# Cross attention: three of four maximum products ahead of the scores, the fourth row strip's scores first, softmax sums copied out of PSUM and divided a step later

## The chip, the cores and the metric

The kernel runs on one core of a Trainium2 chip. The metric is the device time of one execution in microseconds (us), lower is better. Five engines work side by side: TensorE (PE in the profile; its weight loads are PEld), VectorE (DVE), ScalarE (ACT), GpSimd (POOL) and SyncE (SP, which only starts transfers here). They meet through semaphores. TensorE writes to PSUM alone, which has eight banks of 128 partitions x 512 fp32 numbers.

## The reference

The program is a small network on a latent array `x` of 32 batches x 64 rows x 256 channels: cross attention to a context, self attention, a mixture of experts, cross attention again, a Mamba block in two directions and a second feed-forward block. The change touches only the cross attention, which runs twice (as `x0` and `x1`). Cut to what matters, with 16 heads of width 16 and 1601 context rows of 128 channels:

```python
q = (layernorm(x) @ Wq + bq)          # 64 queries in each of 32 batches
k = ctx @ Wk + bk                     # 1601 keys
v = ctx @ Wv + bv
scores = einsum('bhqd,bhkd->bhqk', qh, kh) / sqrt(16)
attn = softmax(scores, axis=-1)
out = einsum('bhqk,bhkd->bhqd', attn, vh)
x = x + concat(out) @ Wo + bo
```

## The kernel before, in words

The 1601 keys of a batch are 13 tiles of 128 (the last has 65), taken two at a time: a batch `u` is seven steps `g` = 0 to 6, and step `s` = 7u + g. Steps 0 to 5 hold two key tiles, step 6 one of 65 keys. A layer has 224 steps.

The softmax is written with keys on the partitions. Its shift, a maximum over keys for each head and query, is therefore made one batch ahead from products with queries on the partitions. Operations are named by a letter:

- **M** (`largest`, L476): the product of rounded queries with 512 rounded keys of the next batch, one for each of four row strips `j` of the array (partitions 32j to 32j+31). VectorE takes its maximum (`keep_max`, L692).
- **K** (`project_keys`, L463) and **V** (`project_values`, L494): projections of keys (for the next step's M) and of values (two steps ahead). ScalarE copies them out (L604, L612). GpSimd rounds the copied keys (`round_keys`, L654) before an M may use them, and splits the context (`split_context`, L367 and L369).
- **scores** (L544): 16 fp32 products, four for each strip, into four PSUM banks `score_ps`, one bank to a strip; then one product a strip that adds the shift (L550). ScalarE takes the exponential in two halves, strips 0 and 1, then 2 and 3 (L630), with the K copy between the halves and the V copy after them. `score_ps` is not doubled: scores wait for both exponentials of the step before.
- **P** (`weigh`, L526): probabilities times values; VectorE adds the result up (`gather`, L722 and L725).
- **S** (`spread_sums`, L502) at step 1: the softmax sums of the batch before, spread over partitions; VectorE divides by them (`divide`, L707 and L709).
- **T** (`turn_maxes`, L484) at step 6: the shift. **W** (`project_out`, L509), every second batch: the output projection; VectorE adds it to `x` (L714).

All but the scores share four PSUM banks, `misc_ps`, in rotation: an operation takes the bank of the fourth operation before it in the list `ORDER`, and `open_bank` waits until that one has been read, by ScalarE for K and V and by VectorE for the rest. Each engine takes its instructions in written order. The fixed order of TensorE in a full step is: scores, M0, M1, K, V, M2, M3, P.

```python
def bank(op):
    return misc_ps[:, AT[op] % NMB, :]
if AT[op] >= NMB:
    read_out(pe, ORDER[AT[op] - NMB])
```

Of the kernel before, what the change touches and what calls it, by code (L numbers as in the profile page):

```python
# [261 lines left out]
def cross_attention(nc, tag, x_sb, ident, x_sel, pair_mask, ctxT, wq, wk, wv, wo, bq, bv, bo):  # L262
# [15 lines left out]
    def cols(i):  # L278
        return slice(i * P, i * P + keys(i))
# [13 lines left out]
    def step_ops(s):  # L293

        u, g = divmod(s, NG)
        early = QUADS if g == NG - 1 else QUADS // 2
        maxima = [("M", u + 1, g, j) for j in range(QUADS)] if u + 1 < B else []
        ops = maxima[:early]
        if key_share(u, g)[0] < B:
            ops.append(("K",) + key_share(u, g))  # L300
        if s + 2 < STEPS:
            ops.append(("V", s + 2))
        ops += maxima[early:]
        if g == NG - 1 and u + 1 < B:
            ops.append(("T", u + 1))
        if s > 0:
            ops.append(("P", s - 1))
        if g == 1 and u > 0:
            ops.append(("S", u - 1))
        if g == 2 and u % 2 == 0 and u > 0:  # L310
            ops.append(("W", u // 2 - 1))
        return ops
# [10 lines left out]
    with ExitStack() as ctx:  # L323
# [75 lines left out]
        u_sb = sb(f"{tag}_u", [P, 2, GROUPS, LQ])  # L399
        oT = sb(f"{tag}_oT", [P, GROUPS, 2, LQ])  # L400
        recip = sb(f"{tag}_recip", [P, GROUPS * LQ])
        bias = sb(f"{tag}_bias", [P, D])
# [12 lines left out]
        score_ready = [sem(f"{tag}_score_ready{ph}") for ph in range(2)]  # L415
        exp_done = sem(f"{tag}_exp_done")
        o_done = sem(f"{tag}_o_done")
        bias_done = sem(f"{tag}_bias_done")
# [23 lines left out]
        def _(pe):  # L442
# [89 lines left out]
            def scores(s):  # L532
# [6 lines left out]
                if s > 0:  # L539
                    pe.wait_ge(exp_done, 2 * s)  # L540
                for n, (h, c) in enumerate(parts):
                    for j in range(QUADS):
                        rows = slice(j * 32, (j + 1) * 32)
                        nc.tensor.matmul(score_ps[0:kn, j, n * P:(n + 1) * P], kT[rows, u % 2, c, cols(mine[h])],  # L544
                                         qz[rows, u % 2, c, :, :].rearrange("p s q -> p (s q)"),
                                         start=n == 0, stop=False, skip_group_check=True)
                if g == 0:
                    read_out(pe, ("T", u))
                for j in range(QUADS):
                    nc.tensor.matmul(  # L550
                        score_ps[0:kn, j, 0:len(mine) * 2 * P], ones[j * 32:j * 32 + 1, 0:kn],
                        shift[j * 32:j * 32 + 1, u % 2, :].rearrange("p (a n) -> p a n", a=1).broadcast_to([1, len(mine), 2 * P]),
                        start=False, stop=True, skip_group_check=True).then_inc(score_ready[j // 2], 1)

            pe.wait_ge(w_in, 16 * NW)
# [14 lines left out]
            for s in range(STEPS):  # L570
                u, g = divmod(s, NG)
                early = QUADS if g == NG - 1 else QUADS // 2
                scores(s)
                if u + 1 < B:
                    for j in range(early):
                        largest(("M", u + 1, g, j))
                if key_share(u, g)[0] < B:
                    project_keys(("K",) + key_share(u, g))
                if s + 2 < STEPS:
                    project_values(("V", s + 2))  # L580
                if u + 1 < B:
                    for j in range(early, QUADS):
                        largest(("M", u + 1, g, j))
                if g == NG - 1 and u + 1 < B:
# [3 lines left out]
                if g == 1 and u > 0:  # L588
                    spread_sums(("S", u - 1))
                if g == 2 and u % 2 == 0 and u > 0:  # L590
                    project_out(("W", u // 2 - 1))
# [93 lines left out]
        def _(dve):  # L685
# [10 lines left out]
            def keep_shift(op):  # L696
# [5 lines left out]
                nc.vector.tensor_copy(shift[:, b % 2, :], bank(op)[:, 0:2 * P]).then_inc(dve_free, 1)  # L702

            def divide(op):
                b = op[1]
                made(dve, op)
                nc.vector.reciprocal(recip[:, :], bank(op)[:, 0:GROUPS * LQ]).then_inc(dve_free, 1)  # L707
                read_out(dve, op)
                nc.vector.tensor_tensor(oT[:, :, b % 2, :], u_sb[:, b % 2, :, :],  # L709
                                        recip[:, :].rearrange("p (r q) -> p r q", q=LQ), ALU.mult).then_inc(o_done, 1)  # L710
# [31 lines left out]
            for s in range(STEPS):  # L742
                u, g = divmod(s, NG)
                if u + 1 < B:
                    for j in range(QUADS):
                        keep_max(("M", u + 1, g, j))
                if g == NG - 1 and u + 1 < B:
                    keep_shift(("T", u + 1))
                if s > 0:
                    gather(("P", s - 1))  # L750
                if g == 1 and u > 0:
                    divide(("S", u - 1))
                if g == 2 and u % 2 == 0 and u > 0:
                    add_out(("W", u // 2 - 1))
            gather(("P", STEPS - 1))
            divide(("S", B - 1))
            add_out(("W", B // 2 - 1))

# [1403 lines left out]
```

## Time and profile before

| | |
|---|---|
| median of 3 runs | 4311.27 us (4309.27 to 4313.52) |
| the profiled execution | 4310.48 us, of it the span 4308.7 us |
| PE busy | 3776.3 us, 88% of the span |
| DVE busy | 2804.7 us, 65% |
| ACT busy | 1979.2 us, 46% |
| POOL busy | 1519.9 us, 35% |
| steps of the first cross attention | 85 to 1143 us of the span |
| steps of the second | 1978 to 3036 us |

An engine's share of busy time is an average over stages that differ. A busy TensorE is not one at its peak, since the records of its products overlap. What matters in a step is which engine's work ends last before the next step can begin.

### The profile page before, as it was taken

What the parts mean: (1) busy time and instruction counts of PE and PEld (TensorE: products, weight loads), DVE (VectorE), ACT (ScalarE), POOL (GpSimd) and SP (SyncE); (2) the same over time, 40 slices, a digit from 0 to 9 for tenths busy, and PEclk for the clock granted to TensorE, in tenths of its full rate; (3) what the DMA queues carried; (4) which work ended last, traced back from release to release, by engine and by line L of the source; (5) the groups of instructions that cost most, each with busy time, mean ns of one, the idle gap of its engine ahead of it and who ended that gap; (6) DMA issues with size and microseconds to landing.
All of it is one profiled execution on the core that took longest, in us unless ns stands there. A gap on an engine that the chain in (4) does not pass through costs nothing. (4 is left out here: it accounts for less than half of the span.)

```text
span 4308.7 us, 129527 instructions
## 1 busy us (share of the span) xinstructions
PE 3776.3 (88%) x54334; PEld 2632.0 (61%) x54335; DVE 2804.7 (65%) x4729; ACT 1979.2 (46%) x2986; POOL 1519.9 (35%) x1445
## 2 busy tenths in 40 slices
PE   6999999999798299948999999999877878878788
PEld 4777777777688166626777777777423333323357
DVE  5666666666466212235666666666779999999964
ACT  2555555555422122214555565555444444444432
POOL 3333323333100200043333333332047777888710
PEclk8999999999899599968999999999979999999989
DMA  1001000000000600120100010000012222222200
GB/s 63 26 26 34 26 26 26 27 33 18 10 0 2 252 28 30 32 71 25 33 26 26 26 32 28 26 26 11 25 49 69 71 72 72 79 76 70 70 33 20
DMA packets 79937, 182.53 MB, mean 42 GB/s; under 512 B 10755, under 2 KB 31267, under 8 KB 79043
## 3 DMA queue, kind: packets, MB, share of 16 engines
q1 hardware_dynamic: 76354, 166.58, 12.3%
q8 instruction: 413, 6.77, 0.6%
q0 software_dynamic: 3072, 8.39, 0.6%
q14 instruction: 98, 0.80, 0.1%
HBM read 157.37 MB, written 17.56 MB: 41 GB/s over the span
## 5 line engine op out<-in xcount | busy, mean ns | idle before, releaser
L692 DVE TENSOR_REDUCE x_maxes<-x_misc_ps 128x1 f32<-128x512 f32 (+1 forms) x1792 | 1044.7, 628 | 569.1 <-PE x_misc_ps L476 568.8
L630 ACT ACTIVATE x_probs<-x_score_ps 128x1024 f32<-128x1024 f32 (+1 forms) x896 | 859.8, 961 | 795.6 <-PE x_score_ps L550 789.2
L654 POOL CAST x_kT_hi<-x_kT 128x512 fp32r<-128x512 f32 (+1 forms) x448 | 257.9, 576 | 1454.3 <-PE x_misc_ps L494 971.1
L1679 PE MATMUL b_acc_ps<-b_read,ident 128*128 128x512 f32 x1024 | 566.1, 683 | 187.3 <-POOL b_read L1765 153.8
L1757 POOL TENSOR_TENSOR b_drive<-b_b_all,b_dtx 128x1024 f32<-128x1024 f32 x256 | 602.5, 2354 | 331.2 <-DVE b_dtx L1837 280.7
L1799 DVE TENSOR_TENSOR_SCAN b_state<-b_decay_ps,b_drive 128x512 f32<-128x512 f32 x512 | 606.7, 1205 | 12.5 <-POOL b_drive L1757 12.5
L1747 ACT ACTIVATE b_decay_ps<-b_dt,b_a_neg 128x504 f32<-128x504 f32 x512 | 350.0, 685 | 461.9 <-DVE b_state L1799 461.9
L1679 PEld LDWEIGHTS b_acc_ps<-b_read,ident 128*128 128x128 f32 x1024 | 193.9, 211 | 505.9 <-POOL b_read L1765 257.2
L544 PE MATMUL x_score_ps<-x_qz,x_kT 32*128 32x128 f32 x13312 | 494.1, 283 | 5.9 <-ACT x_probs L630 5.9
L526 PE MATMUL x_misc_ps<-x_probs,x_v 128*32 128x64 f32 x26624 | 464.8, 221 | 0.5 <-issue 0.5
L526 PEld LDWEIGHTS x_misc_ps<-x_probs,x_v 128*32 128x32 f32 x26624 | 392.6, 110 | 103.8 <-issue 87.6
L544 PEld LDWEIGHTS x_score_ps<-x_qz,x_kT 32*128 32x128 f32 x13312 | 405.5, 182 | 70.6 <-issue 31.2
L476 PE MATMUL x_misc_ps<-x_kT_hi,x_qz_hi 32*128 32x512 f32 (+1 forms) x2048 | 425.9, 400 | 5.1 <-POOL x_kT_hi L654 4.1
L604 ACT ACTIVATE x_kT<-x_misc_ps 128x512 f32<-128x512 f32 (+1 forms) x448 | 247.9, 553 | 158.6 <-PE x_misc_ps L463 155.1
L612 ACT ACTIVATE x_v<-x_misc_ps 128x512 f32<-128x512 f32 (+1 forms) x448 | 255.6, 570 | 12.5 <-PE x_misc_ps L494 12.5
L476 PEld LDWEIGHTS x_misc_ps<-x_kT_hi,x_qz_hi 32*128 32x128 f32 x2048 | 208.1, 186 | 84.3 <-DVE x_maxes L692 21.5
L463 PE MATMUL x_misc_ps<-x_raw_hi,x_wk_hi 128*128 128x512 f32 (+1 forms) x512 | 229.5, 448 | 34.0 <-POOL x_raw_lo L369 15.4
L1809 DVE TENSOR_TENSOR b_read<-b_c_ps,b_state 128x512 f32<-128x512 f32 x384 | 253.7, 661 | 0.0
L494 PE MATMUL x_misc_ps<-x_wv_hi,x_raw_hi 128*128 128x256 f32 (+1 forms) x832 | 241.1, 290 | 0.3
L369 POOL TENSOR_TENSOR x_raw_lo<-x_raw,x_raw_hi 128x512 fp32r<-128x512 f32 (+1 forms) x192 | 235.1, 1225 | 15.5
L494 PE MATMUL x_misc_ps<-x_wv_hi,x_raw_lo 128*128 128x256 f32 (+1 forms) x832 | 233.8, 281 | 0.0
L494 PE MATMUL x_misc_ps<-x_wv_lo,x_raw_hi 128*128 128x256 f32 (+1 forms) x832 | 233.5, 281 | 0.0
(281 smaller groups left out, 5593.3 us busy)
## 6 DMA issues: line engine op xcount, KB each, us to landing
x_raw<-in_ctxT SPq DMA_DIRECT2D x64, 800.5 KB, 4.4
b_b_all<-b_bc_rows SPq DMA_DIRECT2D x128, 256.0 KB, 3.5
b_c_all<-b_bc_rows SPq DMA_DIRECT2D x128, 256.0 KB, 3.1
m_w<-in_m_w SPq DMA_DIRECT2D x16, 704.0 KB, 19.2
m_w<-in_m_w SPq DMA_DIRECT2D x8, 768.0 KB, 19.8
m_slot_rows<-m_zero SPq DMA_DIRECT2D x1, 4992.0 KB, 17.4
m_block_rows<-m_slot_rows SPq DMA_DIRECT2D x39, 128.0 KB, 2.0
m_slot_out<-m_out SPq DMA_DIRECT2D x39, 128.0 KB, 1.7
```

What stands on the lines that cost most here:

```text
L476: ins = nc.tensor.matmul(dst[:, m * kn:(m + 1) * kn], qz_hi[rows, b % 2, c, :, :].rearrange("p s q -> p (s q)"), kT_hi[rows, (b * NG + n) ...
L494: ins = nc.tensor.matmul(dst[0:keys(i), h * D:(h + 1) * D], part[:, b % 2, cols(i)], w[:, :], start=m == 0, stop=m == 2)
L526: ins = nc.tensor.matmul(dst[j * 32:(j + 1) * 32, r * LQ:(r + 1) * LQ], v_sb[0:keys(i), g, h, 8 * c + 2 * j + half, :], probs[0:keys(i), s ...
L544: nc.tensor.matmul(score_ps[0:kn, j, n * P:(n + 1) * P], kT[rows, u % 2, c, cols(mine[h])], qz[rows, u % 2, c, :, :].rearrange("p s q -> p ...
L612: nc.scalar.activation(v_sb[rows, g, 0:n, :, 0:DH].rearrange("p a h d -> p (a h) d"), bank(op)[rows, 0:n * D].rearrange("p (a d) -> p a d" ...
L630: nc.scalar.activation(probs[rows, s % 2, js, 0:n], score_ps[rows, js, 0:n], ACT.Exp).then_inc(exp_done, 1)
L654: nc.gpsimd.tensor_copy(kT_hi[:, at % 2, 0:m * even].rearrange("p (c k) -> p c k", c=m)[:, :, 0:kn], kT[:, b % 2, c:c + m, k0:k0 + kn]).th ...
L692: nc.vector.tensor_reduce(maxes[:, c:c + m, j, k0 // NB], bank(op)[:, 0:m * even].rearrange("p (c k) -> p c k", c=m)[:, :, 0:kn], AX.X, AL ...
L1679: nc.tensor.matmul(acc_ps[:, c, :], ident[:, :], read[:, c, :], start=False, stop=True, skip_group_check=True).then_inc(acc_done, 1)
L1747: nc.scalar.activation(by_sequence(decay_ps[:, c % 2, :])[:, :, inside(p)], by_sequence(dt[:, c, :])[:, :, inside(p)], ACT.Exp, scale=a_ne ...
L1757: nc.gpsimd.tensor_tensor(drive[:, c:c + 2, :], b_all[:, k % 2:k % 2 + 1, :].broadcast_to([P, 2, NB]), dtx[:, c:c + 2, :], ALU.mult).then_ ...
L1799: nc.vector.tensor_tensor_scan(order(state[:, c, :]), order(decay_ps[:, c % 2, :]), order(drive[:, c, :]), 0.0, ALU.mult, ALU.add).then_in ...
```

## The change

On TensorE, M0, M1 and M2 stand ahead of the scores and M3 behind them, ahead of K. Within the scores the last strip (3) has its first two products ahead of those of strips 0 to 2, and its product with the shift earlier, so that it is two products ahead throughout. The wait for the shift's copy at step 0 stands ahead of the scores instead of ahead of L550. `ORDER` changes with it, and so does the operation from whose bank each one must wait. The sums of S are copied from PSUM to SBUF (`keep_sums`, a new operation of VectorE), and the division follows one step later, behind that step's four maxima, from the copy. W moves from step 2 to step 3.

```diff
     def step_ops(s):
 
         u, g = divmod(s, NG)
-        early = QUADS if g == NG - 1 else QUADS // 2
-        maxima = [("M", u + 1, g, j) for j in range(QUADS)] if u + 1 < B else []
-        ops = maxima[:early]
+        ops = [("M", u + 1, g, j) for j in range(QUADS)] if u + 1 < B else []
         if key_share(u, g)[0] < B:
             ops.append(("K",) + key_share(u, g))
         if s + 2 < STEPS:
             ops.append(("V", s + 2))
-        ops += maxima[early:]
...
-        if g == 2 and u % 2 == 0 and u > 0:
+        if g == 3 and u % 2 == 0 and u > 0:
             ops.append(("W", u // 2 - 1))
...
+                for n in range(2):
+                    score(n, late)
+                for n in range(len(parts)):
+                    for j in early:
+                        score(n, j)
+                    if n + 2 < len(parts):
+                        score(n + 2, late)
+                    elif n + 2 == len(parts):
+                        lower(late)
+                for j in early:
+                    lower(j)
...
-                early = QUADS if g == NG - 1 else QUADS // 2
+                if u + 1 < B:
+                    for j in range(QUADS - 1):
+                        largest(("M", u + 1, g, j))
                 scores(s)
                 if u + 1 < B:
-                    for j in range(early):
-                        largest(("M", u + 1, g, j))
+                    largest(("M", u + 1, g, QUADS - 1))
...
+            def keep_sums(op):
+                made(dve, op)
+                nc.vector.tensor_copy(sums[:, :], bank(op)[:, 0:GROUPS * LQ]).then_inc(dve_free, 1)
+
             def divide(op):
                 b = op[1]
-                made(dve, op)
-                nc.vector.reciprocal(recip[:, :], bank(op)[:, 0:GROUPS * LQ]).then_inc(dve_free, 1)
                 read_out(dve, op)
+                nc.vector.reciprocal(recip[:, :], sums[:, :]).then_inc(recip_done, 1)
+                dve.wait_ge(recip_done, b + 1)
...
+                if g == 2 and u > 0:
+                    divide(("S", u - 1))
...
                 if g == 1 and u > 0:
-                    divide(("S", u - 1))
-                if g == 2 and u % 2 == 0 and u > 0:
+                    keep_sums(("S", u - 1))
+                if g == 3 and u % 2 == 0 and u > 0:
                     add_out(("W", u // 2 - 1))
```

TensorE before, in a step 3 of a batch with both W and S (the whole step, from the scores to P; in brackets the semaphores waited for, `act_free` and `dve_free` being the reads of a bank by ScalarE and VectorE):

```order
L544 MATMUL x_score_ps<-x_qz,x_kT 128x128 [waits x0_exp_done]
L544 MATMUL x_score_ps<-x_qz,x_kT 128x128 x15
L550 MATMUL x_score_ps<-x_shift,x_ones 128x512 x4
L476 MATMUL x_misc_ps<-x_kT_hi,x_qz_hi 128x512 [waits x0_kT_hi_done,x0_dve_free] x2
L463 MATMUL x_misc_ps<-x_raw_hi,x_wk_hi 128x512 [waits x0_raw_lo_done,x0_dve_free]
...
L494 MATMUL x_misc_ps<-x_wv_hi,x_raw_lo 128x256
L476 MATMUL x_misc_ps<-x_kT_hi,x_qz_hi 128x512 [waits x0_kT_hi_done,x0_dve_free] x2
L526 MATMUL x_misc_ps<-x_probs,x_v 32x64 [waits x0_act_free,x0_exp_done]
```

TensorE after the change, in the same step 3 of such a batch, from its first maximum product to K:

```order
L475 MATMUL x_misc_ps<-x_kT_hi,x_qz_hi 128x512 [waits x0_kT_hi_done,x0_dve_free]
L475 MATMUL x_misc_ps<-x_kT_hi,x_qz_hi 128x512 [waits x0_kT_hi_done,x0_act_free] x2
L547 MATMUL x_score_ps<-x_qz,x_kT 128x128 [waits x0_exp_done]
L547 MATMUL x_score_ps<-x_qz,x_kT 128x128 x12
L552 MATMUL x_score_ps<-x_shift,x_ones 128x512
L547 MATMUL x_score_ps<-x_qz,x_kT 128x128 x3
L552 MATMUL x_score_ps<-x_shift,x_ones 128x512 x3
L475 MATMUL x_misc_ps<-x_kT_hi,x_qz_hi 128x512 [waits x0_kT_hi_done,x0_dve_free]
L462 MATMUL x_misc_ps<-x_raw_hi,x_wk_hi 128x512 [waits x0_raw_lo_done,x0_dve_free]
```

Two products that wait for a read by ScalarE (the K and the V copy of the step before) now stand ahead of the scores, and no maximum product stands between V and P any more.

VectorE before, from P's read at step 1 to P's read at step 2:

```order
L722 COPY x_u<-x_misc_ps 128x256 [waits x0_misc_ready]
L707 RECIPROCAL x_recip<-x_misc_ps 128x256 [waits x0_misc_ready]
L709 TENSOR_TENSOR x_oT<-x_u,x_recip 128x4x64 [waits x0_dve_free]
L692 TENSOR_REDUCE x_maxes<-x_misc_ps 128x1 [waits x0_misc_ready] x4
L725 TENSOR_TENSOR x_u<-x_misc_ps,x_u 128x256 [waits x0_dve_free,x0_misc_ready]
```

VectorE after the change, the same stretch:

```order
L738 COPY x_u<-x_misc_ps 128x256 [waits x0_misc_ready]
L718 COPY x_sums<-x_misc_ps 128x256 [waits x0_misc_ready]
L704 TENSOR_REDUCE x_maxes<-x_misc_ps 128x1 [waits x0_misc_ready] x4
L723 RECIPROCAL x_recip<-x_sums 128x256 [waits x0_dve_free]
L725 TENSOR_TENSOR x_oT<-x_u,x_recip 128x4x64 [waits x0_recip_done]
L741 TENSOR_TENSOR x_u<-x_misc_ps,x_u 128x256 [waits x0_dve_free,x0_misc_ready]
```

The reciprocal and the multiplication moved behind the four maxima of step 2, and a copy took their place.

## Rows read from the trace of the kernel before

**Rows 1.** Busy time in one stretch: PE, PEld, DVE, ACT, POOL, PEclk, DMA, GB/s

```profile
800.00:1000.00 200.00, 197.62 (x4525) 154.82 (x4524) 130.01 (x236) 117.01 (x168) 63.13 (x90) 1.00 0.09 28
```

**Rows 2.** TensorE in order of time, two batches: start us, duration us, line, records

```profile
484.96 1.17 PE L544 MATMUL x_score_ps<-x_qz,x_kT 32*128 32x128 f32 x32
...
489.11 1.17 PE L544 MATMUL x_score_ps<-x_qz,x_kT 32*128 32x128 f32 x32
...
490.89 0.47 PE L463 MATMUL x_misc_ps<-x_raw_hi,x_wk_hi 128*128 128x512 f32 x1 [0.16 <-POOL x_raw_lo L369]
...
493.91 0.70 PE L502 MATMUL x_misc_ps<-x_u,x_sel 128*128 128x256 f32 x2
494.54 1.17 PE L544 MATMUL x_score_ps<-x_qz,x_kT 32*128 32x128 f32 x32
...
499.57 1.99 PE L509 MATMUL x_misc_ps<-x_wo,x_oT 128*128 128x256 f32 x8
501.50 1.17 PE L544 MATMUL x_score_ps<-x_qz,x_kT 32*128 32x128 f32 x32
502.41 0.50 PE L550 MATMUL x_score_ps<-x_shift,x_ones 1*128 1x512 f32 x4
...
503.05 0.49 PE L463 MATMUL x_misc_ps<-x_raw_hi,x_wk_hi 128*128 128x512 f32 x1
...
504.43 0.28 PE L494 MATMUL x_misc_ps<-x_wv_hi,x_raw_lo 128*128 128x256 f32 x1
...
505.07 1.10 PE L526 MATMUL x_misc_ps<-x_probs,x_v 128*32 128x64 f32 x64
506.10 1.17 PE L544 MATMUL x_score_ps<-x_qz,x_kT 32*128 32x128 f32 x32
...
510.54 1.17 PE L544 MATMUL x_score_ps<-x_qz,x_kT 32*128 32x128 f32 x32
...
515.13 0.67 PE L544 MATMUL x_score_ps<-x_qz,x_kT 32*65 32x128 f32 x16
...
519.27 1.17 PE L544 MATMUL x_score_ps<-x_qz,x_kT 32*128 32x128 f32 x32
...
551.93 1.17 PE L544 MATMUL x_score_ps<-x_qz,x_kT 32*128 32x128 f32 x32
```

**Rows 3.** ScalarE in order of time, from step 3's exponentials to step 4's copy

```profile
503.01 1.03 ACT L630 ACTIVATE x_probs<-x_score_ps 128x1024 f32<-128x1024 f32 x1 [3.92 <-PE x_score_ps L550]
504.04 0.60 ACT L604 ACTIVATE x_kT<-x_misc_ps 128x512 f32<-128x512 f32 x1
504.54 1.02 ACT L630 ACTIVATE x_probs<-x_score_ps 128x1024 f32<-128x1024 f32 x1
505.44 0.61 ACT L612 ACTIVATE x_v<-x_misc_ps 128x512 f32<-128x512 f32 x1
507.61 1.02 ACT L630 ACTIVATE x_probs<-x_score_ps 128x1024 f32<-128x1024 f32 x1 [1.57 <-PE x_score_ps L550]
...
510.04 0.38 ACT L612 ACTIVATE x_v<-x_misc_ps 65x256 f32<-65x256 f32 x1
```

**Rows 4.** All engines in order of time, the last batch of the first layer

```profile
1133.90 1.94 ACT L630 ACTIVATE x_probs<-x_score_ps 128x1024 f32<-128x1024 f32 x2 [1.09 <-PE x_score_ps L550]
...
1134.40 0.28 PE L494 MATMUL x_misc_ps<-x_wv_hi,x_raw_lo 128*128 128x256 f32 x1
1134.62 1.10 PE L526 MATMUL x_misc_ps<-x_probs,x_v 128*32 128x64 f32 x64
...
1135.89 1.17 PE L544 MATMUL x_score_ps<-x_qz,x_kT 32*128 32x128 f32 x32 [0.18 <-ACT x_probs L630]
```

**Rows 5.** VectorE in order of time, the division and the maxima behind it

```profile
494.65 1.76 DVE L707 RECIPROCAL x_recip<-x_misc_ps 128x256 f32<-128x256 f32 x1
496.44 0.42 DVE L709 TENSOR_TENSOR x_oT<-x_u,x_recip 128x256 f32<-128x256 f32 x1
496.78 1.28 DVE L692 TENSOR_REDUCE x_maxes<-x_misc_ps 128x1 f32<-128x512 f32 x2
```

More of the change, by code:

```diff
@@ L400, in cross_attention @@
         oT = sb(f"{tag}_oT", [P, GROUPS, 2, LQ])
+        sums = sb(f"{tag}_sums", [P, GROUPS * LQ])
         recip = sb(f"{tag}_recip", [P, GROUPS * LQ])
@@ L416, in cross_attention @@
         exp_done = sem(f"{tag}_exp_done")
+        recip_done = sem(f"{tag}_recip_done")
         o_done = sem(f"{tag}_o_done")
@@ L540, in scores, with score, lower @@
                     pe.wait_ge(exp_done, 2 * s)
[L541 to L546, printed above, removed]
                 if g == 0:
                     read_out(pe, ("T", u))
-                for j in range(QUADS):
+                *early, late = range(QUADS)
+                def score(n, j):
+                    h, c = parts[n]
+                    rows = slice(j * 32, (j + 1) * 32)
+                    nc.tensor.matmul(score_ps[0:kn, j, n * P:(n + 1) * P], kT[rows, u % 2, c, cols(mine[h])],
+                                     qz[rows, u % 2, c, :, :].rearrange("p s q -> p (s q)"),
+                                     start=n == 0, stop=False, skip_group_check=True)
+                def lower(j):
                     nc.tensor.matmul(
@@ L580, in _ @@
                     project_values(("V", s + 2))
-                if u + 1 < B:
-                    for j in range(early, QUADS):
-                        largest(("M", u + 1, g, j))
                 if g == NG - 1 and u + 1 < B:
@@ L751, in _ @@
                 if g == 1 and u > 0:
-                    divide(("S", u - 1))
-                if g == 2 and u % 2 == 0 and u > 0:
+                    keep_sums(("S", u - 1))
+                if g == 3 and u % 2 == 0 and u > 0:
                     add_out(("W", u // 2 - 1))
             gather(("P", STEPS - 1))
+            keep_sums(("S", B - 1))
             divide(("S", B - 1))
```

## The prediction

> **What bounds the kernel now.** I read first the table of stretches, then TensorE's timeline over two batches, then ScalarE's beside it, and last a place where TensorE has too little to do. In the cross attention TensorE is busy 197.6 of 200 us at the full clock, ScalarE 117 and VectorE 130 [rows 1]. The reader is to see that TensorE has hardly a gap, so that a step lasts as long as its instructions. Times of a step are counted from the start of its scores. Step 3 runs from 501.50 to 506.10, 4.60 us [rows 2]: scores 0.91 to the product with the shift, K at 1.55, the last V product at 2.93, P at 3.57, P itself 1.03.
>
> But ScalarE's chain is as long. From the start of the scores to the first exponential 1.51 us (501.50 to 503.01), then exponential, K copy, exponential, V copy without a gap until 505.44 + 0.61 = 506.05: 3.04 us more [rows 2, 3]. So the V copy ends 4.55 us into a step of 4.60. Today the next scores need only the exponentials, and those are done at 4.06. The last batch, without M and K, shows what a release costs: exponentials end at 1133.90 + 1.94 = 1135.84, scores begin at 1135.89, 0.05 us later [rows 4].
>
> The seven steps of an even batch last 4.15, 5.43, 6.96 (with W), 4.60, 4.44, 4.59 and 4.14 us, together 34.31 (484.96 to 519.27). The odd batch behind it has no W and takes 551.93 - 519.27 = 32.66, the pair 66.97 [rows 2]. There are 15 pairs with all of M, S and W in each of the two layers.
>
> **The change part by part.**
>
> *TensorE's own work.* Scores and L550 use strip 3 as long as strips 0 to 2. M0 to M2 on three strips while strip 3 has its first scores, and M3 on strip 3 while the others end, fill the strips evenly; they take the place of the pair M0, M1 and the way to K stays about 1.5. What goes is the pair M2, M3 between V and P: from the last V product to P are 0.64 us (504.43 to 505.07), and where nothing stands between 0.22 (1134.40 to 1134.62) [rows 2, 4]. That is 0.42 us a step: TensorE would need 4.18.
>
> *The new wait.* By the rotation of four banks M2 gets the bank of the V before it (M1, where an S, T or W stands between). It must wait for ScalarE's V copy and stands ahead of the scores; behind it on TensorE is queued the whole step, and ScalarE then has nothing to do. The loop is closed: scores to V copy's end 4.55, release 0.05, next M2 and with it the scores. A full step cannot be shorter than 4.60 us, whatever TensorE saves. That is just today's length of step 3, and 0.45 more than step 0 takes today.
>
> *Rounded keys.* M0 now needs them at the start of its step. K copy's end lies at 3.14 us (504.64), GpSimd's rounding behind it still fits ahead of 4.60; I take nothing for it.
>
> *The sums.* S and its multiplication stay; the 1.76 us reciprocal and 0.42 us product [rows 5] leave the place between P's read and the maxima. Today they hold up the maxima and with them the banks of step 2: without W it lasts 6.96 - 1.93 = 5.03 us, 0.43 more than step 3 with the same work [rows 2]. That goes. The copy is one VectorE pass over 256 numbers, as the product is, so 0.42. Two such copies at the layers' ends are on the path, 0.8 us. In the new step 2 the division comes behind the maxima: maxima of 0.64 each (1.28 the pair [rows 5]) end near 3.1, reciprocal and product near 5.3, P's addition (0.42) near 5.7, that is 1.1 us into step 3. M3 wants its bank (of the last P) at 1.2, so it passes; M0's maximum starts only then and is read at 1.75, and K, wanted at 1.5, waits about 0.25 for M0's bank. Where ScalarE bounds, K copy is late by 0.15.
>
> *Now each step.* Step 0: 4.60 (ScalarE; today 4.15). Step 1: TensorE 4.18 + S 0.63 (493.91 to 494.54 [rows 2]) = 4.80 (5.43). Today it is 0.20 longer than 4.60 + 0.63; its K waits for GpSimd's split of the context, which is tied to the K copy of step 0 [rows 2]. That copy stays where it is and step 1 begins 0.45 later, so this wait goes too. Step 2: 4.60 (6.96, or about 5.0 in odd batches). Step 3 odd: 4.60 + 0.15 = 4.75 (about 4.6); even, with W of 1.93 (499.57 to 501.50 [rows 2]): 4.18 + 1.93 + 0.25 = 6.35 (4.60). Step 4: V is small; exponential to V copy's end is 507.61 to 510.42, 2.81 [rows 3], so 1.51 + 2.81 + 0.05 = 4.37 (4.44). Step 5: K is small and ScalarE shorter; 4.59 - 0.42 = 4.17. Step 6: all four M are short and no pair stands behind V; the bounds of its gain are nothing and 0.42, and since today M3 there waits for VectorE to read P, which now lies beside the scores, I take 0.3 off: 3.85. Sum even 32.74 (34.31), odd 31.14 (32.66): 3.09 us a pair.
>
> 30 pairs x 3.09 = 92.7; the first batch of each layer, without S, wins 0.7 at steps 5 and 6 and gives 0.45 back at step 0, 0.5 in both layers. Less 0.8 for the copies, 92.4. Against the profiled execution's own 4310.48 that is 4218; the median of the runs is 0.8 above it: 4219 us.
>
> **What the sum does not know.** The trace has no step in which strips hold different kinds of product, nor one strip two products ahead. Lower bound of its cost: nothing, or a gain of up to 0.1 in the scores, since they no longer follow P's differently shaped products directly, and such a change is at most the 0.22 us between the last V product and P, of which I allow half [rows 4]. Eight bound steps a pair, 24 us, thus 4195. Upper bound: the two leading scores hold the other strips back for as long as they take, 8 records of a strip in 0.91 us, thus 4 records 0.45. What do rows say? Each product has two records (32 for 16 products), which need the same strip one after the other; in written order they follow each other directly. If the engine started records strictly in that order, only two strips could ever work abreast, and 32 records would take 1.8 us; they take 0.91 [rows 2]. So records of other strips do pass one that waits for its strip, and I take nothing.
>
> The Trainium skill, TensorE: Matmul & The Clock Gate, "What overlaps and what doesn't", says that matmuls start and end in program order, and only weight loads are pulled ahead. By that rule the early strips' scores would begin three records late. The rows above speak against the strict form of it.
>
> **The rivals.**
>
> *A hold of some 0.2 us.* The strips run apart only a little: the early strips start behind the late strip's first product, or M2 and the scores don't overlap. For: nobody shows how far ahead a record may be taken. 0.22 us more on the chain of steps 0, 2 and 4, about 0.2 at step 5, 0.07 at odd step 3, 0.03 at steps 1 and 6: 1.0 a batch, 1.93 a pair. It leaves 1.16 x 30 = 35 us: 4276.
>
> *Slower: program order holds.* The early strips start after three records of the late one, 0.33 us: 1.73 in the odd and 1.65 in the even batch, 3.38 a pair against 3.09 won: 4320; with the full 0.45 us, 4365. It decides from 0.3 us on, since there the gain is used up. For: the new wait leaves no slack, so each delay of the first exponential counts in full. Against: the 0.91 us.
>
> *It does nothing.* ScalarE bounds as many steps as TensorE does now, so a hold near 0.3 gives 4311.
>
> *Better than the sum*, below 4195: the chain from scores to exponential gets shorter than 1.41, or K and M3 come free at once.
>
> **How the numbers follow.** The forecast 0.58 (4195 to 4250), the small hold 0.20 (4250 to 4295), slower 0.12, nothing 0.05, better 0.05. The likeliest gives 4219. The range 4193 to 4290 leaves out the slower and unchanged cases and a piece on each side. The runs lie within 0.1%, so 0.2% is about what a measurement tells from no change: faster 0.83, within it 0.05, slower 0.12.
>
> **What would show it.** In the changed kernel: P follows the last V product after 0.22 us; a full step is 4.60 us and begins 0.05 us behind the V copy's end; ScalarE waits 1.5 us before the first exponential of steps 0, 2 and 4 and for TensorE each time; step 0 has grown, steps 1, 2, 5 and 6 have shrunk; odd step 3 is 4.75; the reciprocal stands behind the maxima. A pair lasts 63.9 us. It is wrong if scores to first exponential takes much more than 1.51 us, if M0 waits for GpSimd, or if the division holds K of step 3 longer than 0.3.

## The result, and the profile after the change

The changed kernel takes 4238.84 us (median; 4238.59 to 4240.19), the kernel before 4311.56 us (4309.27 to 4313.52). The ratio is 0.9832, with a 95% interval of 0.9815 to 0.9849: 72.7 us faster, where 92 were forecast. 4238.84 lies in the range given.

The page of the changed kernel, busy time of each engine (us, share of the span of 4237.0 us, instructions):

```profile
PE 3695.2 (87%) x54334; PEld 2644.7 (62%) x54335; DVE 2809.9 (66%) x4793; ACT 1946.9 (46%) x2986; POOL 1523.1 (36%) x1445
```

TensorE is 81 us less busy than before and the kernel 72 shorter. One group of the same page shows what TensorE's weight loads for the maximum products were waiting for (busy us, mean ns | idle before, and what ended it):

```profile
L475 PEld LDWEIGHTS x_misc_ps<-x_kT_hi,x_qz_hi 32*128 32x128 f32 x2048 | 257.3, 186 | 159.4 <-ACT x_v L624 62.1
```

A maximum product now waits for ScalarE's V copy (`x_v L624`), 62.1 us in all.

The table of stretches, 800 to 1000 us, answers to [rows 1]:

```profile
800.00:1000.00 200.00, 196.64 (x4716) 161.91 (x4715) 135.82 (x250) 119.31 (x176) 64.87 (x93) 1.00 0.10 32
```

The granted clock is 1.00 in both. TensorE alone still looks like the bound (196.64 of 200 us), and this view can't tell that it isn't: the third maximum product of step 3 is held for half a microsecond, but the records of the two that run ahead (0.50 us each) cover that time, so that it counts as busy. What tells is TensorE's timeline, steps 2 and 3 of an even batch (start, duration, line, records), answering to [rows 2]:

```profile
478.50 0.28 PE L493 MATMUL x_misc_ps<-x_wv_hi,x_raw_lo 128*128 128x256 f32 x1
478.71 1.10 PE L525 MATMUL x_misc_ps<-x_probs,x_v 128*32 128x64 f32 x64
479.74 0.70 PE L501 MATMUL x_misc_ps<-x_u,x_sel 128*128 128x256 f32 x2
480.37 0.50 PE L475 MATMUL x_misc_ps<-x_kT_hi,x_qz_hi 32*128 32x512 f32 x3
480.38 1.16 PE L547 MATMUL x_score_ps<-x_qz,x_kT 32*128 32x128 f32 x26
...
481.52 0.48 PE L552 MATMUL x_score_ps<-x_shift,x_ones 1*128 1x512 f32 x3
...
481.93 0.50 PE L462 MATMUL x_misc_ps<-x_raw_hi,x_wk_hi 128*128 128x512 f32 x1
...
484.56 1.04 PE L475 MATMUL x_misc_ps<-x_kT_hi,x_qz_hi 32*128 32x512 f32 x3
485.11 1.16 PE L547 MATMUL x_score_ps<-x_qz,x_kT 32*128 32x128 f32 x28
...
486.13 0.48 PE L552 MATMUL x_score_ps<-x_shift,x_ones 1*128 1x512 f32 x2
...
486.65 0.50 PE L462 MATMUL x_misc_ps<-x_raw_hi,x_wk_hi 128*128 128x512 f32 x1
```

And ScalarE beside it, answering to [rows 3] (in brackets the idle time before, and what ended it):

```profile
482.13 1.03 ACT L642 ACTIVATE x_probs<-x_score_ps 128x1024 f32<-128x1024 f32 x1 [2.00 <-PE x_misc_ps L475]
483.05 0.59 ACT L616 ACTIVATE x_kT<-x_misc_ps 128x512 f32<-128x512 f32 x1
...
484.43 0.62 ACT L624 ACTIVATE x_v<-x_misc_ps 128x512 f32<-128x512 f32 x1
486.74 1.03 ACT L642 ACTIVATE x_probs<-x_score_ps 128x1024 f32<-128x1024 f32 x1 [1.69 <-PE x_score_ps L552]
487.66 0.59 ACT L616 ACTIVATE x_kT<-x_misc_ps 128x512 f32<-128x512 f32 x1
...
489.05 0.60 ACT L624 ACTIVATE x_v<-x_misc_ps 128x512 f32<-128x512 f32 x1
```

Four things are to be seen. P follows the last V product after 0.21 us (478.50 to 478.71). The V copy ends at 484.43 + 0.62 = 485.05, and the next scores start at 485.11, with the third maximum product (M2) of the group that began at 484.56 held until then: the group lasts 1.04 us instead of 0.50. The step from 480.38 to 485.11 took 4.73 us. And there are two kinds of step start: at 480.37 the step follows TensorE's own work (S), M0 to M2 and the scores start together, and the early strips' products with the shift come 1.14 us after them (481.52); at 485.11 ScalarE released the step, M0 and M1 have run ahead, and it is 1.02 us (486.13). Before it was 0.91 [rows 2].

VectorE at the same place, answering to [rows 5]:

```profile
480.48 0.42 DVE L718 COPY x_sums<-x_misc_ps 128x256 f32<-128x256 f32 x1 [0.17 <-PE x_misc_ps L501]
480.91 2.48 DVE L704 TENSOR_REDUCE x_maxes<-x_misc_ps 128x1 f32<-128x512 f32 x4
483.31 1.74 DVE L723 RECIPROCAL x_recip<-x_sums 128x256 f32<-128x256 f32 x1
485.09 0.42 DVE L725 TENSOR_TENSOR x_oT<-x_u,x_recip 128x256 f32<-128x256 f32 x1
485.43 0.41 DVE L741 TENSOR_TENSOR x_u<-x_misc_ps,x_u 128x256 f32<-128x256 f32 x1
485.76 2.47 DVE L704 TENSOR_REDUCE x_maxes<-x_misc_ps 128x1 f32<-128x512 f32 x4
```

The last batch of the first layer, scores alone, answering to [rows 4]:

```profile
1094.00 1.16 PE L547 MATMUL x_score_ps<-x_qz,x_kT 32*128 32x128 f32 x29 [0.17 <-ACT x_probs L642]
...
1097.62 1.16 PE L547 MATMUL x_score_ps<-x_qz,x_kT 32*128 32x128 f32 x29 [0.17 <-ACT x_probs L642]
```

A step of 3.62 us; before 3.51 (1132.38 to 1135.89, read from the same view of the kernel before). The run with no head start, below, has 3.51 again: 0.11 us is the hold of the two leading products by itself.

In this table a step is the time from one start of the scores to the next, as a mean over batches 2 to 29 of the first layer, worked out from such timelines. E stands for even batches (with W), O for odd ones; "x 30" is the change of the pair against before, times 30 pairs.

```
                    g=0   1     2     3     4     5     6     sum    pair   x 30
before           E  4.15  5.43  6.96  4.60  4.44  4.59  4.14  34.31
                 O  4.18  5.64  5.03  4.63  4.45  4.59  4.14  32.66  66.97
forecast         E  4.60  4.80  4.60  6.35  4.37  4.17  3.85  32.74
                 O  4.60  4.80  4.60  4.75  4.37  4.17  3.85  31.14  63.88   -93
changed          E  4.58  4.81  4.73  6.11  4.49  4.28  4.03  33.03
                 O  4.59  4.82  4.72  4.62  4.39  4.29  3.92  31.35  64.38   -78
division only    E  4.15  5.43  4.61  7.45  4.45  4.58  4.15  34.82
                 O  4.18  5.64  4.65  5.53  4.50  4.59  4.14  33.23  68.05   +32
order only       E  4.58  4.82  7.53  4.72  4.39  4.29  4.02  34.35
                 O  4.58  4.82  6.03  4.62  4.38  4.29  3.91  32.63  66.98     0
no head start    E  4.60  4.95  4.73  6.25  4.50  4.32  4.03  33.38
                 O  4.62  4.95  4.71  4.73  4.50  4.35  3.91  31.77  65.15   -55
one ahead        E  4.58  4.81  4.77  6.11  4.51  4.23  4.02  33.03
                 O  4.58  4.83  4.87  4.62  4.38  4.23  3.93  31.44  64.47   -75
two and two      E  4.16  5.02  4.20  6.48  4.18  4.17  3.93  32.14
                 O  4.19  5.22  4.19  4.57  4.18  4.18  3.81  30.34  62.48  -135
  product later  E  4.16  5.00  4.21  6.10  4.18  4.17  3.90  31.72
                 O  4.18  5.21  4.21  4.21  4.17  4.18  3.80  29.96  61.68  -159
P ahead of V     E  4.41  5.22  5.22  6.13  4.42  4.28  4.15  33.83
                 O  4.40  5.41  5.21  4.38  4.43  4.29  4.15  32.27  66.10   -26
```

The steps account for the time: the two attention layers last 1020.0 and 1017.6 us instead of 1057.9 and 1057.3, 77.6 less. The rest of the program came out 5.8 us longer in this execution (2199.3 instead of 2193.5 us), of which the copies of the sums at the layers' ends were forecast to take 0.8. In the ten traces of this study the rest takes 2191.7 to 2199.3 us whatever the order of the attention, so that a few microseconds of it are the spread of executions. What makes the spread is open.

Step 5 is the last thing to read here, because its bound has changed. TensorE and ScalarE at its start and at its end:

```profile
495.70 1.16 PE L547 MATMUL x_score_ps<-x_qz,x_kT 32*128 32x128 f32 x28
...
499.84 0.42 PE L475 MATMUL x_misc_ps<-x_kT_hi,x_qz_hi 32*128 32x66 f32 x3
499.98 0.32 PE L547 MATMUL x_score_ps<-x_qz,x_kT 32*65 32x128 f32 x1
```

```profile
499.30 0.61 ACT L624 ACTIVATE x_v<-x_misc_ps 128x512 f32<-128x512 f32 x1
```

TensorE is done with P and starts the next maxima at 499.84, 4.14 us into the step, but the scores start at 499.98, 0.07 us after the V copy's end (499.91). So ScalarE's chain bounds step 5 too, with 4.28 us.

### The profile page after: what moved, and what is told of

The parts are those of the page before. It is cut to its first block and busy times, and to the rows that moved or that the text cites. A ratio compares the mean times of both kernels' runs of the same rounds, so it can differ in the third digit from the quotient of the medians.

```text
span 4237.0 us, 129595 instructions
## 1 busy us (share of the span) xinstructions
PE 3695.2 (87%) x54334; PEld 2644.7 (62%) x54335; DVE 2809.9 (66%) x4793; ACT 1946.9 (46%) x2986; POOL 1523.1 (36%) x1445
## 5 line engine op out<-in xcount | busy, mean ns | idle before, releaser
L704 DVE TENSOR_REDUCE x_maxes<-x_misc_ps 128x1 f32<-128x512 f32 (+1 forms) x1792 | 1015.2, 625 | 57.8 <-PE x_misc_ps L475 54.6
L547 PE MATMUL x_score_ps<-x_qz,x_kT 32*128 32x128 f32 x13312 | 577.8, 280 | 5.0 <-ACT x_probs L642 5.0
L475 PE MATMUL x_misc_ps<-x_kT_hi,x_qz_hi 32*128 32x512 f32 (+1 forms) x2048 | 507.6, 422 | 36.1 <-POOL x_kT_hi L666 28.1
L547 PEld LDWEIGHTS x_score_ps<-x_qz,x_kT 32*128 32x128 f32 x13312 | 491.0, 181 | 7.5 <-ACT x_probs L642 6.6
L741 DVE TENSOR_TENSOR x_u<-x_misc_ps,x_u 128x256 f32<-128x256 f32 x384 | 162.5, 423 | 381.5 <-PE x_misc_ps L525 381.5
L475 PEld LDWEIGHTS x_misc_ps<-x_kT_hi,x_qz_hi 32*128 32x128 f32 x2048 | 257.3, 186 | 159.4 <-ACT x_v L624 62.1
L552 PE MATMUL x_score_ps<-x_shift,x_ones 1*128 1x512 f32 (+1 forms) x1792 | 300.1, 458 | 0.0
L624 ACT ACTIVATE x_v<-x_misc_ps 128x512 f32<-128x512 f32 (+1 forms) x448 | 257.8, 575 | 11.8 <-PE x_misc_ps L493 11.8
```

Source lines behind the costliest of these rows:

```text
L475: ins = nc.tensor.matmul(dst[:, m * kn:(m + 1) * kn], qz_hi[rows, b % 2, c, :, :].rearrange("p s q -> p (s q)"), kT_hi[rows, (b * NG + n) ...
L552: nc.tensor.matmul(score_ps[0:kn, j, 0:len(mine) * 2 * P], ones[j * 32:j * 32 + 1, 0:kn], shift[j * 32:j * 32 + 1, u % 2, :].rearrange("p ...
L624: nc.scalar.activation(v_sb[rows, g, 0:n, :, 0:DH].rearrange("p a h d -> p (a h) d"), bank(op)[rows, 0:n * D].rearrange("p (a d) -> p a d" ...
L704: nc.vector.tensor_reduce(maxes[:, c:c + m, j, k0 // NB], bank(op)[:, 0:m * even].rearrange("p (c k) -> p c k", c=m)[:, :, 0:kn], AX.X, AL ...
```

## The experiments

The theory was the prediction's: TensorE no longer has the pair M2, M3 between V and P (0.42 us a step), and a wait for the V copy stands ahead of the scores, so that ScalarE's chain sets a floor of 4.6 us. Each experiment's ratio is to the kernel before, run on the same chip. The changed kernel was run once more beside the last three:

> The changed kernel again, beside the others: 4239 +- 3. Both theories expect the same of it.

It took 4236.57 us (4234.39 to 4240.43), ratio 0.9827 (0.9814 to 0.984): the same result.

**The division alone.** The kernel before, with the division moved and nothing else:

```diff
-        if g == 2 and u % 2 == 0 and u > 0:
+        if g == 3 and u % 2 == 0 and u > 0:
             ops.append(("W", u // 2 - 1))
...
+                if g == 2 and u > 0:
+                    divide(("S", u - 1))
...
                 if g == 1 and u > 0:
-                    divide(("S", u - 1))
+                    keep_sums(("S", u - 1))
```

> The kernel before with only the second half of the change: the softmax sums are copied out of their bank at step 1, the division follows behind the maxima of step 2, W stands at step 3. My theory: the 2.2 us of reciprocal and product only change their place on VectorE. Step 2 loses its 0.43 us, but the division then holds P's read, and with it the banks of step 3 (V and the last maxima there wait for VectorE), for about as long; near 4311, within 4295 to 4325. Rival (the move of the division carries the gain by itself): 60 batches x 0.43 = 26 us or more, 4285 or less.

4342.79 us (4340.77 to 4346.14), ratio 1.0076 (1.0059 to 1.0092): slower by 31, outside what either theory gave. Step 2 falls by 0.4 us as forecast (5.03 to 4.65 in odd batches), but step 3 grows by 0.9 (4.63 to 5.53). VectorE and TensorE of this kernel at the same place, from the end of step 2 into step 3:

```profile
469.56 1.74 DVE L713 RECIPROCAL x_recip<-x_sums 128x256 f32<-128x256 f32 x1
471.34 0.43 DVE L715 TENSOR_TENSOR x_oT<-x_u,x_recip 128x256 f32<-128x256 f32 x1
471.68 0.42 DVE L731 TENSOR_TENSOR x_u<-x_misc_ps,x_u 128x256 f32<-128x256 f32 x1
```

```profile
472.15 0.38 PE L496 MATMUL x_misc_ps<-x_wv_hi,x_raw_hi 128*128 128x256 f32 x1 [0.35 <-DVE x_u L731]
```

P's addition (L731) stands behind the division. In the old order V of step 3 takes the bank of P and waits for it, and everything behind V waits too. In the changed order that bank goes to M3, which is wanted late enough. So the division's move needs the new `ORDER`. The P of an odd step 3 starts 4.50 us after its scores instead of 3.60, V 0.60 late and the maxima behind it waiting for VectorE as well.

**The new order alone.** The changed kernel with the old division at step 1 and W at step 2:

```diff
             def divide(op):
                 b = op[1]
+                made(dve, op)
+                nc.vector.reciprocal(recip[:, :], bank(op)[:, 0:GROUPS * LQ]).then_inc(dve_free, 1)
                 read_out(dve, op)
-                nc.vector.reciprocal(recip[:, :], sums[:, :]).then_inc(recip_done, 1)
-                dve.wait_ge(recip_done, b + 1)
...
                 if g == 1 and u > 0:
-                    keep_sums(("S", u - 1))
+                    divide(("S", u - 1))
```

> The changed kernel with only the first half of the change: maxima ahead of the scores and the late strip, but the reciprocal again straight from the bank at step 1 and W at step 2. My theory: the division (2.2 us) then lies ahead of the first maximum of step 2, in whose bank K of that step goes; K starts about 1.4 us late instead of without a wait, and ScalarE's second exponential waits for the K copy: 1.0 to 1.3 us on each of 60 batches, 60 to 78 us back: 4295 to 4320. Rival (the order of the maxima carries the gain alone, the division is a detail): 4230 to 4260.

4315.88 us (4311.81 to 4317.16), ratio 1.0009 (0.9999 to 1.0018), as expected: no gain. Step 2 of an odd batch takes 6.03 us, against 4.72 in the changed kernel. TensorE's timeline in this kernel shows where:

```profile
496.49 0.49 PE L474 MATMUL x_misc_ps<-x_kT_hi,x_qz_hi 32*128 32x512 f32 x1 [0.29 <-DVE x_recip L718]
...
497.55 0.49 PE L461 MATMUL x_misc_ps<-x_raw_hi,x_wk_hi 128*128 128x512 f32 x1 [0.57 <-DVE x_maxes L703]
```

M3 waits until the reciprocal has read S's bank, and K for the first maximum behind the division. K starts 2.97 us after the scores (494.58) instead of 1.55. So the halves alone give +31 and +4 us, of which the 4 can't be told from nothing, and together -73: each move takes away what makes the other cost.

**No head start for the fourth strip.** The changed kernel with the scores in the old order:

```diff
-                for n in range(2):
-                    score(n, late)
                 for n in range(len(parts)):
-                    for j in early:
+                    for j in range(QUADS):
                         score(n, j)
-                    if n + 2 < len(parts):
-                        score(n + 2, late)
```

> The changed kernel with the scores in their old order: strip by strip for each product, all four shift products last; the fourth strip has no head start. My theory: records of the free strip pass those that wait for strips 0 to 2 anyway, so the head start is not needed, and it costs 0.11 us where ScalarE bounds, since the early strips' shift products end 1.02 instead of 0.91 us after the scores' start. In the last batch of each layer steps fall from 3.62 to 3.51. About 3.5 bound steps a batch x 0.11 x 60 = 23 us less: 4216 (4205 to 4232). Rival (the head start is what lets maxima and scores overlap): the scores come 0.2 us later in each TensorE-bound step, 4250 to 4290.

4256.9 us (4254.69 to 4259.09), ratio 0.9874 (0.9857 to 0.989): 18 us slower than the changed kernel. I had expected no loss or a gain. The rival's range holds, but not its reason: the scores do not come 0.2 us late. A step that the V copy opens, to be compared with the changed kernel's from 485.11:

```profile
490.33 1.16 PE L546 MATMUL x_score_ps<-x_qz,x_kT 32*128 32x128 f32 x29
...
491.99 0.50 PE L462 MATMUL x_misc_ps<-x_raw_hi,x_wk_hi 128*128 128x512 f32 x1
```

The first exponential comes 1.54 us after the scores, earlier than the 1.63 of the changed kernel. But the last strip is ready later, M3 behind it starts at 491.67 (1.34 us; changed 1.22), and K at 1.66 instead of 1.54. ScalarE's K copy waits for K (492.99, that is 2.66 instead of 2.55), and the V copy ends 4.66 us into the step instead of 4.54. So steps 1, 3, odd 4 and 5 lose 0.04 to 0.14 us, step 0 0.02 or 0.03. Steps 2 and, in even batches, 4, which TensorE's own work opens, lose at most 0.01: there the first exponential comes at 1.73 or 1.75 in either kernel, and K is not what ScalarE waits for.

Such a step also shows what one product can do when others ahead of it wait. The maxima hold strips 0 to 2:

```profile
485.59 0.50 PE L475 MATMUL x_misc_ps<-x_kT_hi,x_qz_hi 32*128 32x512 f32 x3
485.62 1.26 PE L546 MATMUL x_score_ps<-x_qz,x_kT 32*128 32x128 f32 x29
```

In the trace's single records one product of the scores starts at 485.62, and three more at 485.92 and 485.93, 0.34 us after the maxima began. The early one can only be that of the free strip 3, although the three of strips 0 to 2 stand ahead of it in the program. So a product does pass others that wait for their strip. Its strip is still 0.12 us later with M3: counted from the maxima, its first record is 0.02 us later than in the changed kernel, and the two records of its second product stand 0.21 us apart instead of 0.11. Why they do is not shown.

**One product ahead instead of two.**

```diff
-                for n in range(2):
-                    score(n, late)
+                score(0, late)
...
-                    if n + 2 < len(parts):
-                        score(n + 2, late)
-                    elif n + 2 == len(parts):
-                        lower(late)
+                    if n + 1 < len(parts):
+                        score(n + 1, late)
+                lower(late)
```

> The changed kernel with the fourth strip one product ahead of the others instead of two. The run e3_plain showed that no head start costs 0.14 us in steps that TensorE bounds. My theory: the 0.11 us by which the other strips' shift products end late is what their first records wait behind four records of the fourth strip; with two records ahead it is gone or smaller (last batch 3.51 to 3.56 instead of 3.62), and one product is enough to keep the fourth strip busy beside three maxima of the same length, 0.21 us: 4220 to 4236. Rival (the head start has to be two products): between the changed kernel and e3_plain, 4240 to 4257.

4236.13 us (4233.2 to 4239.01), ratio 0.9823 (0.9809 to 0.9836): no difference from the changed kernel that can be told. It lies at the upper edge of what I had expected. The last batch, where nothing but scores, V and P stand in a step, measures what the head start costs. Two starts of the scores there:

```profile
1094.94 1.17 PE L547 MATMUL x_score_ps<-x_qz,x_kT 32*128 32x128 f32 x32 [0.21 <-ACT x_probs L640]
...
1098.48 1.17 PE L547 MATMUL x_score_ps<-x_qz,x_kT 32*128 32x128 f32 x32 [0.21 <-ACT x_probs L640]
```

A step is 3.51 to 3.52 us with none ahead (1102.36 to 1105.88 in that kernel), 3.54 with one, 3.62 with two. The full steps do not become shorter by this, and ScalarE shows why. A step of this kernel that the V copy opens:

```profile
485.98 1.17 PE L547 MATMUL x_score_ps<-x_qz,x_kT 32*128 32x128 f32 x30
```

```profile
487.54 1.03 ACT L640 ACTIVATE x_probs<-x_score_ps 128x1024 f32<-128x1024 f32 x1 [1.62 <-PE x_score_ps L552]
488.53 0.60 ACT L614 ACTIVATE x_kT<-x_misc_ps 128x512 f32<-128x512 f32 x1
```

The first exponential comes 1.56 us after the scores instead of 1.63 (485.11 to 486.74). But the K copy stands 2.55 us behind the scores in both (485.98 to 488.53, 485.11 to 487.66), since K's last product ends only then (488.50 and 487.62), and the V copy ends at 4.56 and 4.54. Up to about 1.63 the first exponential is not what the chain waits for. Only step 5, whose K is short, gets shorter, from 4.28 to 4.23. That would be 3 us in all. In this execution a few odd steps 2 of 5.0 to 6.0 us (mean 4.87 instead of 4.72) took most of it back; they are not explained.

**The wait off the scores' way.** If the V copy's wait is what bounds a full step, its product must stand behind the scores. The maxima of strips 2 and 3 come first, plain scores, then the maxima of strips 0 and 1. The first of these two takes the V copy's bank, except behind an S, T or W, where it is still the second maximum ahead of the scores:

```diff
+    TURN = (2, 3, 0, 1)
...
                 if u + 1 < B:
-                    for j in range(QUADS - 1):
+                    for j in TURN[:2]:
                         largest(("M", u + 1, g, j))
                 scores(s)
                 if u + 1 < B:
-                    largest(("M", u + 1, g, QUADS - 1))
+                    for j in TURN[2:]:
+                        largest(("M", u + 1, g, j))
```

with `TURN` in `ORDER` and on VectorE too, and no head start.

> Maxima of strips 2 and 3 ahead of the scores, scores in plain order, maxima of strips 0 and 1 behind them, ahead of K; the rest as in the changed kernel. The V copy's bank is now taken by the third maximum, behind the scores, so that scores wait again for the exponentials alone. My theory (ScalarE's whole chain, closed by the wait for the V copy, is the floor of a step now): a full step falls from 4.6 to TensorE's own 4.2, step 0 from 4.58 to about 3.8; some 2 us a batch, 60 batches: 4120 (4095 to 4150). Rival (the floor is ScalarE's work or VectorE's reads, not the place of that wait): 4205 to 4240.

4179.74 us (4174.09 to 4182.51), ratio 0.9698 (0.9682 to 0.9714): 59 us faster than the changed kernel, and outside both expectations: the place is right, the size was taken too large. TensorE and ScalarE of this kernel at step 4:

```profile
476.55 1.16 PE L547 MATMUL x_score_ps<-x_qz,x_kT 32*128 32x128 f32 x28
...
480.71 1.16 PE L547 MATMUL x_score_ps<-x_qz,x_kT 32*128 32x128 f32 x29
```

```profile
480.49 0.38 ACT L619 ACTIVATE x_v<-x_misc_ps 65x256 f32<-65x256 f32 x1
```

The next scores start at 480.71, before this V copy has ended (480.87), and the step is 4.16 us. Full steps are 4.18 to 4.20, TensorE's own 4.18 of the prediction. The edit changes two more things. The head start is gone, which by itself cost 18 us in the changed kernel. And the maxima ahead stand on strips 2 and 3, so that strips 0 and 1 are free for the first exponential: it comes at 1.53 us in step 2 instead of 1.75. How the 59 us divide among the three was not measured, but the step above shows the wait itself gone.

What the expected size left out is first the exponentials. The end of a step 0 that began at 456.68:

```profile
459.73 1.02 ACT L637 ACTIVATE x_probs<-x_score_ps 128x1024 f32<-128x1024 f32 x1
```

```profile
460.73 0.59 PE L476 MATMUL x_misc_ps<-x_kT_hi,x_qz_hi 32*128 32x512 f32 x2 [0.24 <-POOL x_kT_hi L661]
460.86 1.16 PE L547 MATMUL x_score_ps<-x_qz,x_kT 32*128 32x128 f32 x29
```

They end at 460.75, 4.07 us into the step, and the next scores need both. So step 0 could not fall to 3.8, even if the next M, which GpSimd's rounding holds until 460.73, were earlier; it lasts 4.16 to 4.19, as before the change. The rest stands in the table of waits, 200 to 1000 us (total, times, longest):

```profile
PEld x_misc_ps L463 <- DVE x_maxes L699: 25.6, 52, 0.7
...
PE x_misc_ps L463 <- POOL x_raw_lo L367: 4.8, 14, 0.4
```

K waits for a maximum, at step 3 for one that stands behind the division; and step 1's K waits for GpSimd's split of the context, a wait that the changed kernel had hidden by its longer step 0.

**The product of the division later.** The reciprocal stays, the multiplication by it moves behind the maxima of step 3:

```diff
+            def apply(op):
+                b = op[1]
                 dve.wait_ge(recip_done, b + 1)
...
+                if g == 3 and u > 0:
+                    apply(("S", u - 1))
```

> The kernel of the run e4_two_two with the division split: the reciprocal stays behind the maxima of step 2, the product with it (0.42 us) goes behind the maxima of step 3. My theory: step 3 lasts 4.57 us there against 4.20 of a full step, because K waits for the bank of the step's first maximum, which VectorE starts late; 0.42 us less ahead of it takes 0.3 to 0.4 off step 3, 60 times: 18 to 24 us below e4_two_two, 4155 to 4162. Rival (step 3 waits for something else, the context or W): no change, 4175 to 4182.

4151.99 us (4147.22 to 4154.21), ratio 0.9627 (0.9612 to 0.9641), 28 us less: a little more than expected (the two profiled executions differ by 22). Step 3 falls from 4.57 to 4.21 and from 6.48 to 6.10, and no other step moves. This is the fastest version of the study.

**P ahead of V.** The other way to lift the wait: in the changed kernel V goes behind P, so that the V copy is not the last thing that TensorE needs:

```diff
-        if s + 2 < STEPS:
-            ops.append(("V", s + 2))
...
             ops.append(("P", s - 1))
+        if s + 2 < STEPS:
+            ops.append(("V", s + 2))
```

> The changed kernel with one thing moved on TensorE: P (at step 6 T and P) stands ahead of V instead of behind it. Maxima, scores, head start and division stay as changed. The bank of V is then taken by the fourth maximum, behind the scores, in the steps that follow no S or W; the third takes that of P. My theory (the wait for the V copy ahead of the scores makes ScalarE's whole chain the floor): full steps behind steps without S and W fall from 4.61 to 4.2 to 4.25 us; steps 2, and 4 in even batches, keep it; 4185 to 4210. Rival (ScalarE's work or the head start is the floor): 4230 to 4245.

4289.0 us (4288.57 to 4290.66), ratio 0.9947 (0.9932 to 0.9963): 52 us slower than the changed kernel, and outside both expectations. Where ScalarE bounded, steps do fall (step 0 from 4.58 to 4.41, odd step 3 from 4.62 to 4.38), not as far as the 4.2 expected, which is left open. But steps 1 and 2 grow to 5.2 or more. In step 1 the old wait is still there and comes later: M2 of the next step takes the V copy's bank there, and as V now follows P, its copy ends only at 490.83, the scores of step 2 starting at 490.88. Step 2 has a new wait. TensorE's timeline at the start of step 3, and one row of the waits of 200 to 1000 us:

```profile
495.28 0.50 PE L475 MATMUL x_misc_ps<-x_kT_hi,x_qz_hi 32*128 32x512 f32 x2
496.08 0.49 PE L475 MATMUL x_misc_ps<-x_kT_hi,x_qz_hi 32*128 32x512 f32 x1 [0.30 <-DVE x_u L741]
496.09 1.16 PE L547 MATMUL x_score_ps<-x_qz,x_kT 32*128 32x128 f32 x28
```

```profile
PEld x_misc_ps L475 <- DVE x_u L741: 23.3, 48, 0.7
```

The rotation gives M2 the bank of P now, and P the bank of a maximum. Both are read by VectorE, and after the division VectorE is late: M2, ahead of the scores, waits 0.8 us for P's addition (495.28 to 496.08). So the wait for ScalarE was made later at step 1 and exchanged for a worse one at step 2.

## Why the prediction was right, and where its terms were off

**What goes on TensorE.** Right: V to P is 0.21 us instead of 0.64. That the full step is then 4.18 of TensorE's own work is shown where nothing else bounds it (4.18 to 4.20 with two and two).

**The new wait.** Right, and tested: scores follow the V copy's end by 0.06 us, step 0 grew to 4.58, and in the kernel whose scores start before the V copy has ended the full step is 4.18 to 4.20. It is the reason why 4.18 on TensorE did not become 4.18 a step.

**The sums.** Right: the reciprocal stands behind the maxima, step 2 of odd batches falls from 5.03 to 4.72, and without the move there is no gain at all. Step 3's wait for a bank was overrated: 6.11 and 4.62 us instead of 6.35 and 4.75. P's addition ends at 485.84, 0.73 us into step 3 where 1.1 was forecast: VectorE's instructions start before the one ahead has ended (485.09, 485.43 and 485.76, though the first two last 0.42 and 0.41 us), and step 2 itself is longer. So K starts at 486.65, 1.54 us into step 3, as in the other steps: it is not held at all. 6.11 is 4.18 and W's 1.93.

**Rounded keys and the context's split.** The split's wait went, as forecast (step 1 is 4.81 against 4.80). The rounded keys, taken at nothing, do hold M0 in some steps: 9.1 us in 37 waits of up to 0.3 us, from 200 to 1000 us. Where I looked (M0 held until 495.36) the scores still followed the V copy's end (495.64, scores 495.70), so it was not on the path there.

**"1.51 us to the first exponential", and "I take nothing" for the head start.** These are the terms that were mis-sized. Where the V copy opens a step, the two leading products hold the other strips by 0.11 us (1.02 against 0.91 to the shift; 3.62 against 3.51 in the last batch), and the first exponential comes at 1.63 (485.11 to 486.74). Where TensorE's own work opens it, in steps 2 and even 4, the figure is 1.75 (480.38 to 482.13). This is another cost, which the prediction does not name: the maxima start together with the scores, on the strips that the first exponential needs. It is there without a head start too (1.73), and gone where the maxima stand on strips 2 and 3 (1.53).

**"3.04 us more" to the V copy's end.** This term held 0.11 us of waiting for K, which the prediction took for work: before, the K copy starts 1.03 us after the first exponential (503.01 to 504.04), since K's last product ends only at 504.01; in the changed kernel, where K is ready, 0.92 (482.13 to 483.05), and the whole term is 2.92 (482.13 to 485.05). So the first exponential can be 0.11 us later at no cost, and that is what the hold cost in steps 0, 1 and odd 3: nothing. In steps 2 and even 4 half of the 0.24 is left (1.75 + 2.92 + 0.06 = 4.73). In step 5 K is short, the chain had no such slack, and the 0.11 counts in full: 4.28 instead of 4.17. The prediction had step 5 bound by TensorE; it is bound by ScalarE.

**Luck.** The forecast lies near the result partly because of this slack, which it did not know of. Without it the same delays would have cost 0.11 or 0.12 us more at seven steps of a pair (0, 2 and 4 in both batches, 3 in the odd one), by this estimate some 24 us.

**What records may pass.** The conclusion that a record can pass others that wait for their strip held for the one case that a trace shows (485.62 against 485.92, no head start). That nothing is lost by it did not: without the head start the kernel is 18 us slower.

**The sum.** A pair lasts 64.4 us, not 63.9: step 2 +0.13 (even) and +0.12 (odd), step 4 +0.12 and +0.02, step 5 +0.11 and +0.12, step 6 +0.18 and +0.07, against -0.24 and -0.13 at step 3. That is 0.50 x 30 = 15 of the 20 us missed; the other 5 are the rest of the program, within the spread of executions. Step 6 was a choice between bounds of nothing and 0.42, and the runs showed 0.11 (even) and 0.22 (odd) where 0.3 was taken. Outside the pairs the first batches, forecast to win 0.5 us together, lost 0.8: the first step of the first layer took 6.25 us instead of 4.53, and from 84 to 90 us the granted clock was 0.50 instead of 0.84.

The rivals "program order holds", "it does nothing" and "better than the sum" are out: the hold is 0.11 us, below the 0.3 at which the gain would have been used up. "A hold of some 0.2 us" had the size of the delay in steps 2 and even 4 about right, but took it for the strips running apart, and in full.

## What to carry to other kernels

With a fixed rotation of banks, the order on one engine decides whose read each product waits for. Put the product that waits for the other engine's last copy behind the work that this engine needs next; merely moving it forward turns that engine's chain into the floor of the step. Of two moves one can lose alone (+31 us here) and the other do nothing (+4, within the noise), and together they win (-73), so a half that fails is no verdict on the whole. When a reordering takes a wait away, look for the operation that inherits the bank, and at how late its reader is.

## What the hardware showed that I had not expected

- One product on a free row strip started 0.03 us after the maxima and 0.31 us ahead of three products that stand before it in the program and wait for their strips (485.62 against 485.92, no head start).
- Two leading products on one strip held the three other strips by 0.11 us, one by about 0.03 (last batch: 3.62 and 3.54 against 3.51 us).
- A product that is held can leave no idle time on the profile: M2 stood until 485.10, but the records of M0 and M1 cover the time, and TensorE reads 98% busy (196.64 of 200 us) in steps that ScalarE bounds.
- The first exponential could be 0.07 us earlier (1.56 instead of 1.63) and the V copy ended no sooner, as the K copy between them waited for K's products.
